# Top-k attention in a hybrid block on Trainium2: one rotation of PSUM pairs, a hold of three slots, six of ten masks on POOL, and checks in groups of three tiles

## The chip, the cores and the metric

One NeuronCore of a Trainium2 chip runs the whole program in one launch. The metric is device time in microseconds (us), lower is better; times given are medians of several executions. Engine names: PE is TensorE (PEld its weight loads), DVE is VectorE, ACT is ScalarE, POOL is GpSimd, SP is SyncE, which issues the DMAs.

## The reference, cut to what matters

The input is 8 images of 64 channels by 56 x 56, so 3136 tokens each. A deformable convolution comes first, then a two-layer top-k self-attention on the 3136 tokens of each image (8 heads of 8 channels, so 64 heads a layer), then a mixture of experts. The change touches the attention alone:

```python
scores = einsum('bhqd,bhkd->bhqk', q, kk) * scale     # 3136 x 3136 per head
vals, idx = top_k(scores, 32)                         # the 32 largest of each row
w = softmax(vals)
out = einsum('bhqk,bhqkd->bhqd', w, take_along_axis(v, idx))
```

## The kernel before, in words

The rows (queries) of a head are cut into 25 tiles of 128 (the last has 64). `heads` runs `attend` in a device loop over blocks of 8 heads: 8 blocks a layer, two layers, so 16 blocks, 128 heads and 3200 tiles. Inside a block each engine has its instructions written out in one fixed order, and semaphores tie the engines together.

A tile goes through these steps:

- **Scores.** PE makes the 3136 scores of the tile in four pieces (`scores`, L271): 2, 2, 2 and 1 matmuls of 448 columns, each piece into the same two PSUM banks 0 and 1. ACT copies each piece to the SBUF ring `S` (`keep`, L400), which holds 8 tiles. PE waits for that copy before the next piece.
- **Selection.** DVE takes the 8 largest of each of 28 chunks of 112 scores (`part_top`, 28 MAX8, L489). Between these, at every second chunk k, it runs one step for the tile before (`candidates`): MAX8 and MATCH_REPLACE8 on 92 candidates (L508 to L521). L521 leaves the 32nd largest score, and its semaphore `found` says so. L525 writes whether a row of the tile may have been selected wrongly.
- **Mask.** A 0/1 mask "score below the threshold" of 128 x 3136 in fp8 is made by the engine that the string `MAKERS` names for tile number mod 10: "D" is one DVE TENSOR_SCALAR right behind L525 (L531), "P" is two POOL instructions after `found`, a comparison into `B` (L214) and a cast into `Z` (L219). `Z` has 10 slots; a mask waits until the mask ten tiles earlier has been read by PE (`mask_freed`).
- **Check.** For a group of tiles (`CHECKS`) PE adds up the doubts into PSUM (`flag`, L279), DVE reads them (L541, L542), loads the maximum into a register and branches. If it isn't zero, DVE searches each flagged tile anew in full rows (`search`, L559 to L566). Until a group is checked its tiles stay in `S`, and the fills that use them wait (`s_free`).
- **Values.** A set is four tiles of queries (512 columns; the seventh set of a head has one tile). For each pair of key tiles, a unit, PE fills two PSUM banks with scores turned round less the row maximum, and adds the masks times a large negative number (`fill`, L309 and L318). ACT takes the exponential (`exps`, L430), PE multiplies with the values (`values`, L354). Units alternate between banks 2 and 3 and banks 4 and 5. The row maxima come by `shift_parts` on POOL (L231 to L236, six small instructions a set, or a tile for the last set), `shifts` on PE and `shift_rows` on ACT.

The order: a block has 800 score pieces (slots) and 640 units, and `units_at(a)` puts 0.8 units behind each slot. Three sets of each block's last head are left over for the next block. PE runs one piece and two units ahead of ACT. The check of a group with last tile L is read by DVE in tile L + 3 at chunk k = 7 (`LATE` is 3), and PE issues its flag before the first piece of tile L + 4. A block ends when every engine has ended.

Of the kernel before, what the change touches and what calls it, by code (L numbers as in the profile page):

```python
# [18 lines left out]
CW = 448  # L19
NC = TOK // CW  # L20
NT = -(-TOK // 128)
# [41 lines left out]
RANKED = TOP_AT + 8 * CHUNKS  # L63
RING = 8
MASKS = 10
MAKERS = "DPDDPDDPDD"
BLOCK = 8
PIECES = (2, 2, 2, 1)
AP = len(PIECES)
# [1 line left out]
SETS = -(-TOK // QW)  # L71
PER_HEAD = 6 * 13 + 2
PENDING = 4
CHECKS = [range(4 * g, 4 * g + 4) for g in range(5)] + [range(20, NT)]
LATE = 3
BEHIND = 4
TERMS, ZERO_TO, MAX_AT = 48, 96, 96


# [26 lines left out]
def attend(nc, m, base, n):  # L106
# [4 lines left out]
    with semaphores(nc, *names) as sems, nc.Block() as block:  # L111
# [10 lines left out]
        units = [(s, p) for s, (i, g) in enumerate(sets) for p in range(len(set_pieces(g)))]  # L122
        NE = len(units)
        SLOTS = NA if n else NE
        first_unit = [next(e for e, (s, _) in enumerate(units) if s == k) for k in range(len(sets))] + [NE]
        batch = [sum(batch_ends(sets[s][1], p) for s, p in units[:e]) for e in range(NE + 1)]

        fold_at = [min(first_unit[s + 1] + 3, first_unit[s + 2]) for s in range(len(sets) - 1)]

        def units_at(a):  # L130

            return range(-(-a * NE // SLOTS), -(-(a + 1) * NE // SLOTS))

        def units_through(i):

# [117 lines left out]

        @block.tensor
        def _(pe):
            def scores(a):
                tile, c = divmod(a, AP)
                i, t = divmod(tile, NT)
                if c == 0:
                    for k in range(len(CHECKS)):  # L260
                        before = tile - LATE - 1 - CHECKS[k][-1]
                        if before >= 0 and before % NT == 0:
                            flag(before // NT, k)
                if t == 0 and c == 0 and i >= 1:
                    pe.wait_ge(q_in, 96 * i)
                if a >= 1:
                    pe.wait_ge(a_ev, a)
                rows = tile_rows(t)
                for j in range(PIECES[c]):
                    at = CW * (sum(PIECES[:c]) + j)  # L270
                    mm = pe.matmul(bank[j][0:rows, 0:CW], m.Q[0:ZERO_TO, side(i), 128 * t:128 * t + rows],  # L271
                                   m.K[0:ZERO_TO, side(i), at:at + CW], start=True, stop=True)
                mm.then_inc(a_mm, 1)

# [18 lines left out]
            def fill(e):  # L293

                s, p = units[e]
                i, g = sets[s]
                w = set_width(g)
                per = QW // w
                if p == 0 and i >= 0:
                    pe.wait_ge(max_in, max_sets(i) + g + 1)  # L300
                    pe.wait_ge(s_free, checks_to(i, set_tiles(g)[-1]))
                    masks_made(pe, NT * i + set_tiles(g)[-1])
                if e >= 2:
                    pe.wait_ge(e_exp, e - 1)

                def shifted(x, k):
                    rows = tile_rows(k)
                    at = w * (x % per)
                    pe.matmul(bank[2 + 2 * (e % 2) + x // per][0:rows, at:at + w],  # L309
                              m.K[0:MAX_AT + 3, side(i), 128 * k:128 * k + rows],  # L310
                              m.Q[0:MAX_AT + 3, side(i), QW * g:QW * g + w], start=True, stop=False)

                def masked(x, k):
                    rows = tile_rows(k)
                    for j, t in enumerate(set_tiles(g)):
                        cols = tile_rows(t)
                        at = w * (x % per) + 128 * j
                        mm = pe.matmul(bank[2 + 2 * (e % 2) + x // per][0:rows, at:at + cols],  # L318
                                       mask_at(NT * i + t)[:, 128 * k:128 * k + rows], m.NEG[:, 0:cols],
                                       start=False, stop=(j == len(set_tiles(g)) - 1))  # L320
                    return mm

                tiles = list(enumerate(set_pieces(g)[p]))
                if per == 1:
                    for x, k in tiles:
                        shifted(x, k)
                    for x, k in tiles:
                        mm = masked(x, k)
                else:
                    for x, k in tiles:  # L330
                        shifted(x, k)
                        mm = masked(x, k)
                mm.then_inc(e_mm, 1)
# [29 lines left out]
                    pe.wait_ge(os_done, s)  # L363
                pe.matmul(psX[0:9, 0:w], m.fold[:, :], m.O4[:, 0:w], start=True, stop=True).then_inc(fold_mm, 1)

            if NA:
                scores(0)
            fill(0)
            fill(1)
            for a in range(SLOTS):  # L370
                if a + 1 < NA:
                    scores(a + 1)
                for e in units_at(a):
                    if e + 2 < NE:
                        fill(e + 2)
                    if e + 4 in first_unit and e + 4 < NE and sets[units[e + 4][0]][0] >= 0:
                        shifts(*sets[units[e + 4][0]])
                    if e in fold_at:
                        fold(fold_at.index(e))
                    if batch_ends(sets[units[e][0]][1], units[e][1]):  # L380
                        values(e)
            for s in range(len(sets)):
                if s == len(sets) - 1 or fold_at[s] >= NE:
                    fold(s)
# [6 lines left out]
        def _(act):  # L391
            def keep(a):
                tile, c = divmod(a, AP)
                i, t = divmod(tile, NT)
                rows, at, w = tile_rows(t), CW * sum(PIECES[:c]), PIECES[c]
                act.wait_ge(a_mm, a + 1)
                if c == 0 and tile >= RING:
                    act.wait_ge(s_free, checks_to(*divmod(tile - RING, NT)))
                    masks_made(act, tile - RING)
                act.copy(m.S[0:rows, slot(tile), at:at + CW * w].rearrange("p (a n) -> p a n", a=w),  # L400
                         m.AB[0:rows, 0:w, 0:CW]).then_inc(a_ev, 1)

            def mask(tile):
                i, t = divmod(tile, NT)
                rows = tile_rows(t)
                act.wait_ge(found, tile + 1)
                if mask_freed(tile):
                    act.wait_ge(e_mm, mask_freed(tile))
                act.activation(mask_at(tile)[0:rows, :], m.S[0:rows, slot(tile), :], ACT.Relu,
                               bias=m.M8[0:rows, side(i), t, 31:32], scale=-1.0).then_inc(z_act, 1)  # L410

            def shift_rows(i, g):
                k = max_sets(i) + g
# [4 lines left out]
            def exps(e):  # L418
                s, p = units[e]
                i, g = sets[s]  # L420
                w = set_width(g)
                tiles, per = set_pieces(g)[p], QW // w
                b = 2 + 2 * (e % 2)
                act.wait_ge(e_mm, e + 1)
                if e >= 4:
                    act.wait_ge(pv, batch[e - 4] + 1)
                whole = [k for k in tiles if tile_rows(k) == 128]
                n_banks = len(whole) // per
                if n_banks:
                    ins = act.activation(m.W[:, e % 4, 0:n_banks, :], m.AB[:, b:b + n_banks, :], ACT.Exp)  # L430
                if len(whole) < len(tiles):
                    rows = tile_rows(tiles[-1])
                    ins = act.activation(m.W[0:rows, e % 4, n_banks, 0:w], m.AB[0:rows, b + n_banks, 0:w], ACT.Exp)  # L433
                ins.then_inc(e_exp, 1)
# [12 lines left out]
                    act.wait_ge(o_out, 16 * (s - 1))  # L447
                act.copy(m.OS[:, s % 2, 0:w], psX[0:9, 0:w]).then_inc(os_done, 1)

            for a in range(SLOTS):  # L450
                if a < NA:
                    keep(a)
                    if a % AP == AP - 1 and a >= AP * BEHIND and maker(a // AP - BEHIND) == "A":
                        mask(a // AP - BEHIND)
                for e in units_at(a):
                    exps(e)
                    if e + 3 in first_unit and e + 3 < NE and sets[units[e + 3][0]][0] >= 0:
                        shift_rows(*sets[units[e + 3][0]])
                    if e - 1 in first_unit[1:]:
                        sums(first_unit.index(e - 1) - 1)  # L460
                    if e - 5 in first_unit[1:]:
                        folded(first_unit.index(e - 5) - 1)
            for tile in range(max(TILES - BEHIND, 0), TILES):
                if maker(tile) == "A":
                    mask(tile)
            sums(len(sets) - 1)
            for s in range(len(sets)):
                if first_unit[s + 1] + 5 >= NE:
# [6 lines left out]
        def _(dve):  # L475
# [93 lines left out]
            for tile in range(TILES):  # L569
                steps = candidates(tile - 1) if tile else []  # L570
                for k in range(CHUNKS):
                    checked = False
                    for g in range(len(CHECKS)):
                        before = tile - LATE - CHECKS[g][-1]
                        if k == 7 and before >= 0 and before % NT == 0:
                            check(before // NT, g)
                            checked = True
                    part_top(tile, k, checked)
# [1310 lines left out]
```

## Time and profile before

| what | value |
|---|---|
| median of 3 runs | 39696.92 us (39691.07 to 39698.17) |
| profiled execution | 39708.52 us, its span 39706.6 us |
| busy | DVE 82%, PE 70%, ACT 54%, POOL 34% |
| mean granted TensorE clock | 0.842 |

The span is the time from the first to the last instruction. Busy time counts an engine's instructions, not its waits on semaphores or its branches. A granted clock of 1.0 is 2.4 GHz, 0.5 is 1.2 GHz. In a timeline, instructions of one line that stand next to each other are merged, with their count; the duration of an instruction overlaps with the start of the next, so distances between starts say more than durations.

### The profile page before, as it was taken

To read this page: it belongs to the slowest core of one execution; us is meant where nothing else is said; L and a number is where in the kernel's file an instruction comes from. 1 tells how busy PE (TensorE), PEld (TensorE's weight loads), DVE (VectorE), ACT (ScalarE), POOL (GpSimd) and SP (SyncE) were. 2 spreads that over 40 slices of the span, in tenths; PEclk is the share of its full clock that TensorE was granted. 3 is DMA by queue.
4 is the path that set the end of the run, shared out by engine and by line. 5 is a ranking of instruction groups with operands and counts; after the bars stand their busy time and mean duration, and the time that the engine had idled before them with its cause. 6 is when DMAs were issued, how large, how long until landed. Compare 5 with 4: busy or idle time off the path is not lost. (4 is left out here: it accounts for less than half of the span.)

```text
span 39706.6 us, 613726 instructions
## 1 busy us (share of the span) xinstructions
PE 27975.2 (70%) x190808; PEld 12251.7 (31%) x190809; DVE 32620.3 (82%) x145784; ACT 21431.0 (54%) x28193; POOL 13534.3 (34%) x7470
## 2 busy tenths in 40 slices
PE   5557776676877767877357677777776777774399
PEld 4533332222333323333123233333332333331122
DVE  5659999999999999999669998989999989996611
ACT  1126665555766656666146566666665666663111
POOL 0004443333444434434024344444443444441000
PEclk7779898888989889989579899999988999896555
DMA  0010000000000000000110000000000000001100
GB/s 37 8 51 5 5 5 4 4 5 4 6 5 5 5 4 6 5 5 5 51 51 5 5 5 5 5 5 5 5 5 4 5 5 5 5 5 42 55 10 7
DMA packets 133124, 454.27 MB, mean 11 GB/s; under 512 B 29244, under 2 KB 85444, under 8 KB 111240
## 3 DMA queue, kind: packets, MB, share of 16 engines
q1 hardware_dynamic: 129256, 410.72, 3.1%
q8 instruction: 1448, 23.72, 0.2%
q14 instruction: 2420, 19.82, 0.2%
HBM read 244.71 MB, written 165.93 MB: 10 GB/s over the span
## 5 line engine op out<-in xcount | busy, mean ns | idle before, releaser
L489 DVE MAX8 C<-S 128x8 f32<-128x112 f32 x89600 | 18969.8, 265 | 1146.0 <-issue 775.5
L400 ACT COPY S<-banks 128x896 f32<-128x896 f32 (+1 forms) x12800 | 10429.5, 815 | 10738.9 <-PE banks L271 7966.3
L214 POOL TENSOR_SCALAR B<-S,M 128x3136 bf16<-128x3136 f32 (+1 forms) x960 | 7894.6, 8224 | 15675.9 <-DVE M L521 15675.9
L271 PE MATMUL banks<-K,Q 96*128 96x448 bf16 x22400 | 6725.9, 371 | 5675.5 <-ACT S L400 5170.6
L430 ACT ACTIVATE W<-banks 128x1024 f32<-128x1024 f32 (+1 forms) x9524 | 9810.9, 1030 | 72.0 <-PE banks L318 71.7
L309 PE MATMUL banks<-Q,K 99*128 99x512 bf16 (+2 forms) x22550 | 6593.2, 378 | 2133.0 <-ACT W L430 2059.6
L354 PE MATMUL banks<-W,V 128*32 128x512 f32 (+1 forms) x45100 | 7188.5, 604 | 145.3 <-ACT W L433 106.2
L318 PE MATMUL banks<-NEG,Z 128*128 128x128 bf16 (+3 forms) x80450 | 6717.5, 227 | 0.0
L318 PEld LDWEIGHTS banks<-NEG,Z 128*128 128x128 fp8e4 (+1 forms) x80450 | 5846.5, 103 | 2570.5 <-issue 463.8
L271 PEld LDWEIGHTS banks<-K,Q 96*128 96x128 bf16 x22400 | 1470.7, 99 | 12174.3 <-ACT S L400 7731.6
L531 DVE TENSOR_SCALAR Z<-S,M 128x3136 fp8e4<-128x3136 f32 (+1 forms) x2240 | 4694.9, 2096 | 31.1 <-PE banks L318 31.1
L219 POOL CAST Z<-B 128x3136 fp8e4<-128x3136 bf16 (+1 forms) x960 | 3693.0, 3847 | 138.9 <-POOL B L214 8.5
L309 PEld LDWEIGHTS banks<-Q,K 99*128 99x128 bf16 (+1 forms) x22550 | 1787.9, 103 | 5384.2 <-ACT W L430 3745.9
L517 DVE MATCH_REPLACE8 C<-M,C 128x92 f32<-128x92 f32 x9600 | 2266.6, 236 | 2.3 <-issue 0.5
L516 DVE MAX8 M<-C 128x8 f32<-128x92 f32 x9600 | 2262.2, 236 | 1.7
L354 PEld LDWEIGHTS banks<-W,V 128*32 128x32 f32 x45100 | 1284.3, 114 | 1080.6 <-issue 508.1
L1734 DVE TENSOR_TENSOR moe_hw<-moe_hg,banks 128x448 f32<-128x448 f32 x448 | 278.4, 621 | 1514.1 <-ACT moe_hg L1667 1514.1
L865 PE MATMUL banks<-dc_tap,c_group 128*128 128x224 f32 x2800 | 777.0, 362 | 789.5 <-DVE dc_tap L920 789.5
L541 DVE CAST FI<-banks 1x4 int32<-1x4 f32 (+1 forms) x768 | 118.9, 155 | 1376.4 <-PE banks L279 1373.9
L1667 ACT ACTIVATE moe_hg<-banks,moe_b 128x448 f32<-128x448 f32 x448 | 284.0, 634 | 1563.9 <-PE banks L1629 1563.9
L885 ACT ACTIVATE dc_d<-banks,c_omb 128x224 f32<-128x224 f32 x378 | 149.6, 448 | 1801.5 <-PE banks L854 1801.3
L561 DVE MAX8 M<-S 128x8 f32<-128x3136 f32 (+1 forms) x297 | 1018.0, 3427 | 23.8 <-issue 2.3
(200 smaller groups left out, 21734.9 us busy)
## 6 DMA issues: line engine op xcount, KB each, us to landing
q<-ln_o SPq DMA_DIRECT2D x20, 1568.0 KB, 5.1
ln_x<-y SPq DMA_DIRECT2D x16, 1568.0 KB, 6.0
K<-k_parts SPq DMA_DIRECT2D x130, 147.0 KB
Q<-q_parts SPq DMA_DIRECT2D x130, 147.0 KB
q_parts<-pj_parts SPq DMA_DIRECT2D x24, 784.0 KB, 4.7
k_parts<-pj_parts SPq DMA_DIRECT2D x24, 784.0 KB, 7.8
V<-v_rows SPq DMA_DIRECT2D x130, 112.5 KB, 7.4
v_rows<-pj_vt SPq DMA_DIRECT2D x8, 1800.0 KB, 11.8
```

The lines of the kernel that those rows point to most:

```text
L214: chained(lambda: pool.tensor_scalar(m.B[0:rows, :], m.S[0:rows, slot(tile), :], m.M8[0:rows, side(i), t, 31:32], None, ALU.is_lt))
L219: pool.tensor_copy(mask_at(tile)[0:rows, :], m.B[0:rows, :], saturate=False).then_inc(z_pool, 1)
L271: mm = pe.matmul(bank[j][0:rows, 0:CW], m.Q[0:ZERO_TO, side(i), 128 * t:128 * t + rows], m.K[0:ZERO_TO, side(i), at:at + CW], start=True, ...
L309: pe.matmul(bank[2 + 2 * (e % 2) + x // per][0:rows, at:at + w], m.K[0:MAX_AT + 3, side(i), 128 * k:128 * k + rows], m.Q[0:MAX_AT + 3, sid ...
L318: mm = pe.matmul(bank[2 + 2 * (e % 2) + x // per][0:rows, at:at + cols], mask_at(NT * i + t)[:, 128 * k:128 * k + rows], m.NEG[:, 0:cols], ...
L354: mm = pe.matmul(psO[32 * (k % 4):32 * (k % 4) + 32, 0:w], m.V1[0:rows, side(i), k, :], m.W[0:rows, at, x // per, w * (x % per):w * (x % p ...
L400: act.copy(m.S[0:rows, slot(tile), at:at + CW * w].rearrange("p (a n) -> p a n", a=w), m.AB[0:rows, 0:w, 0:CW]).then_inc(a_ev, 1)
L430: ins = act.activation(m.W[:, e % 4, 0:n_banks, :], m.AB[:, b:b + n_banks, :], ACT.Exp)
L489: ins = dve.max(m.C[0:rows, tile % 2, TOP_AT + k:RANKED:CHUNKS], m.S[0:rows, slot(tile), CHUNK * k:CHUNK * k + CHUNK])
L516: steps.append(lambda r=r: chained(lambda: dve.max(top(r), few)))
L517: steps.append(lambda r=r: chained(lambda: dve.match_replace(few, top(r), few, LOW)))
L531: dve.tensor_scalar(mask_at(tile)[0:rows, :], m.S[0:rows, slot(tile), :], m.M8[0:rows, side(i), t, 31:32], None, ALU.is_lt, saturate=False ...
```

## The change

The scores and the units no longer have banks of their own. `works` lists pieces and units in the order in which ACT takes them, and work w uses banks 2(w mod 3) and the next one; PE produces work w + 3 when work w has been read. The units of a block stand three slots later (`HOLD`). `MAKERS` goes from 3 POOL masks in ten to 6. Checks go from six groups of four tiles a head (the last of five) to eight of three (the last of four), are read at chunk k = 14, and their flag is issued before the third piece of tile L + 3. ACT's own mask path, which no letter of `MAKERS` used, is gone.

```diff
-MAKERS = "DPDDPDDPDD"
+MAKERS = "DPPDPDPPDP"
-CHECKS = [range(4 * g, 4 * g + 4) for g in range(5)] + [range(20, NT)]
+CHECKS = [range(3 * g, 3 * g + 3) for g in range(7)] + [range(21, NT)]
 LATE = 3
-BEHIND = 4
+HOLD = 3
+PAIRS_ = 3
...
+        DELAY = HOLD if n else 0
...
         def units_at(a):
-
-            return range(-(-a * NE // SLOTS), -(-(a + 1) * NE // SLOTS))
+            a -= DELAY
+            return range(-(-max(a, 0) * NE // SLOTS), -(-max(a + 1, 0) * NE // SLOTS))
+
+        works = []
+        for a in range(SLOTS + DELAY):
+            works += [("score", a)] * (a < NA) + [("value", e) for e in units_at(a)]
...
+        def pair(w):
+            return 2 * (w % PAIRS_)
...
+            def freed(w):
+                if w >= PAIRS_:
+                    kind, x = works[w - PAIRS_]
+                    pe.wait_ge(a_ev if kind == "score" else e_exp, x + 1)
...
-                if c == 0:
+                if c == 2:
                     for k in range(len(CHECKS)):
-                        before = tile - LATE - 1 - CHECKS[k][-1]
+                        before = tile - LATE - CHECKS[k][-1]
...
-                if a >= 1:
-                    pe.wait_ge(a_ev, a)
+                freed(score_at[a])
...
-                if e >= 2:
-                    pe.wait_ge(e_exp, e - 1)
+                freed(value_at[e])
...
+            for w in range(PAIRS_):
+                produce(w)
+            for w, (kind, e) in enumerate(works):
+                produce(w + PAIRS_)
+                if kind == "value":
                     if e in fold_at:
                         fold(fold_at.index(e))
                     if batch_ends(sets[units[e][0]][1], units[e][1]):
                         values(e)
+                    if e + 5 in first_unit and e + 5 < NE and sets[units[e + 5][0]][0] >= 0:
+                        shifts(*sets[units[e + 5][0]])
...
-                        if k == 7 and before >= 0 and before % NT == 0:
+                        if k == 14 and before >= 0 and before % NT == 0:
```

## Rows read from the trace of the kernel before

**Rows 1.** The page, part 5: groups by line; busy us, mean ns, idle before.

```profile
L489 DVE MAX8 C<-S 128x8 f32<-128x112 f32 x89600 | 18969.8, 265 | 1146.0 <-issue 775.5
L531 DVE TENSOR_SCALAR Z<-S,M 128x3136 fp8e4<-128x3136 f32 (+1 forms) x2240 | 4694.9, 2096 | 31.1 <-PE banks L318 31.1
L561 DVE MAX8 M<-S 128x8 f32<-128x3136 f32 (+1 forms) x297 | 1018.0, 3427 | 23.8 <-issue 2.3
```

**Rows 2.** Waits of the whole span: total us, times, longest.

```profile
ACT S L400 <- PE banks L271: 7966.3, 7064, 3.8
PE banks L271 <- ACT S L400: 5170.6, 3452, 81.0
DVE FI L541 <- PE banks L279: 1373.9, 612, 5.7
DVE C L489 <- ACT S L400: 250.8, 184, 10.8
```

**Rows 3.** Line L489 in each layer: count, min/median/max ns, first and last start.

```profile
L489 DVE MAX8 C<-S x44800: 252/265/288, 2884.4 to 18845.5; 128x8 f32<-128x112 f32 x192, 64x8 f32<-64x112 f32 x8
...
L489 DVE MAX8 C<-S x44800: 252/265/288, 20383.3 to 36103.4; 128x8 f32<-128x112 f32 x192, 64x8 f32<-64x112 f32 x8
```

**Rows 4.** Busy time by engine in one stretch of attention.

```profile
25000.00:30000.00 5000.00, 3862.75 (x28852) 1639.27 (x28852) 4567.38 (x22242) 3309.55 (x4238) 2191.15 (x1218) 0.92 0.02 5
```

**Rows 5.** DVE timeline, two thresholds, a POOL-masked and a DVE-masked tile, a check.

```profile
26362.38 0.24 DVE L521 MAX8 M<-C 128x8 f32<-128x92 f32 x1
...
26369.08 0.24 DVE L521 MAX8 M<-C 128x8 f32<-128x92 f32 x1
...
26370.12 2.46 DVE L531 TENSOR_SCALAR Z<-S,M 128x3136 fp8e4<-128x3136 f32 x1
...
26377.20 0.14 DVE L542 TENSOR_REDUCE FI<-banks 1x1 int32<-1x4 f32 x1
26378.53 0.28 DVE L489 MAX8 C<-S 128x8 f32<-128x112 f32 x1 [1.19 <-issue]
...
26382.51 1.83 DVE L531 TENSOR_SCALAR Z<-S,M 128x3136 fp8e4<-128x3136 f32 x1
26384.26 1.51 DVE L489 MAX8 C<-S 128x8 f32<-128x112 f32 x8
```

**Rows 6.** POOL timeline beside it, and the cast of an earlier mask.

```profile
26315.28 2.80 POOL L219 CAST Z<-B 128x3136 fp8e4<-128x3136 bf16 x1
...
26362.72 8.21 POOL L214 TENSOR_SCALAR B<-S,M 128x3136 bf16<-128x3136 f32 x1 [17.45 <-DVE M L521]
26371.06 4.16 POOL L219 CAST Z<-B 128x3136 fp8e4<-128x3136 bf16 x1
26375.20 0.23 POOL L231 TENSOR_SCALAR R<-M 128x4 f32<-128x4 f32 x1
...
26376.56 0.19 POOL L236 CAST P<-R 128x4 bf16<-128x4 f32 x1
```

**Rows 7.** POOL timeline where a mask came late.

```profile
8581.59 8.23 POOL L214 TENSOR_SCALAR B<-S,M 128x3136 bf16<-128x3136 f32 x1 [11.40 <-DVE M L521]
8589.95 2.80 POOL L219 CAST Z<-B 128x3136 fp8e4<-128x3136 bf16 x1
```

**Rows 8.** DVE timeline in the same place.

```profile
8590.09 4.30 DVE L531 TENSOR_SCALAR Z<-S,M 128x3136 fp8e4<-128x3136 f32 x1 [1.01 <-PE banks L318]
```

**Rows 9.** DVE timeline of a search.

```profile
25174.63 0.14 DVE L542 TENSOR_REDUCE FI<-banks 1x1 int32<-1x4 f32 x1
...
25205.75 0.28 DVE L489 MAX8 C<-S 128x8 f32<-128x112 f32 x1 [2.81 <-issue]
```

**Rows 10.** DVE timeline at the end of a block.

```profile
26268.88 0.25 DVE L521 MAX8 M<-C 64x8 f32<-64x92 f32 x1
...
26281.61 1.52 DVE L489 MAX8 C<-S 128x8 f32<-128x112 f32 x8 [8.37 <-ACT S L400]
```

**Rows 11.** POOL timeline there, its last instruction of the block.

```profile
26272.40 0.19 POOL L236 CAST P<-R 128x1 bf16<-128x1 f32 x1
```

More of the change, by code:

```diff
@@ L130, in units_at @@
         def units_at(a):
-            return range(-(-a * NE // SLOTS), -(-(a + 1) * NE // SLOTS))
+            a -= DELAY
[3 more added lines that the diff above has]
+            works += [("score", a)] * (a < NA) + [("value", e) for e in units_at(a)]
+        score_at = {x: w for w, (kind, x) in enumerate(works) if kind == "score"}
+        value_at = {x: w for w, (kind, x) in enumerate(works) if kind == "value"}
+        def pair(w):
+            return 2 * (w % PAIRS_)
         def units_through(i):
@@ L270, in scores @@
                     at = CW * (sum(PIECES[:c]) + j)
-                    mm = pe.matmul(bank[j][0:rows, 0:CW], m.Q[0:ZERO_TO, side(i), 128 * t:128 * t + rows],
+                    mm = pe.matmul(bank[pair(score_at[a]) + j][0:rows, 0:CW], m.Q[0:ZERO_TO, side(i), 128 * t:128 * t + rows],
                                    m.K[0:ZERO_TO, side(i), at:at + CW], start=True, stop=True)
@@ L302, in fill @@
                     masks_made(pe, NT * i + set_tiles(g)[-1])
-                if e >= 2:
-                    pe.wait_ge(e_exp, e - 1)
+                freed(value_at[e])
+                b = pair(value_at[e])
                 def shifted(x, k):
@@ L308, in shifted @@
                     at = w * (x % per)
-                    pe.matmul(bank[2 + 2 * (e % 2) + x // per][0:rows, at:at + w],
+                    pe.matmul(bank[b + x // per][0:rows, at:at + w],
                               m.K[0:MAX_AT + 3, side(i), 128 * k:128 * k + rows],
@@ L317, in masked @@
                         at = w * (x % per) + 128 * j
-                        mm = pe.matmul(bank[2 + 2 * (e % 2) + x // per][0:rows, at:at + cols],
+                        mm = pe.matmul(bank[b + x // per][0:rows, at:at + cols],
                                        mask_at(NT * i + t)[:, 128 * k:128 * k + rows], m.NEG[:, 0:cols],
@@ L364, in fold, with produce @@
                 pe.matmul(psX[0:9, 0:w], m.fold[:, :], m.O4[:, 0:w], start=True, stop=True).then_inc(fold_mm, 1)
[L366 to L377, printed above, removed]
+            def produce(w):
+                if w < len(works):
+                    kind, x = works[w]
+                    if kind == "score":
+                        scores(x)
+                    else:
+                        fill(x)
+            for w in range(PAIRS_):
[3 more added lines that the diff above has]
+                if kind == "value":
                     if e in fold_at:
@@ L400, in keep @@
                 act.copy(m.S[0:rows, slot(tile), at:at + CW * w].rearrange("p (a n) -> p a n", a=w),
[L401 to L410, printed above, removed]
+                         m.AB[0:rows, pair(score_at[a]):pair(score_at[a]) + w, 0:CW]).then_inc(a_ev, 1)
             def shift_rows(i, g):
@@ L422, in exps @@
                 tiles, per = set_pieces(g)[p], QW // w
-                b = 2 + 2 * (e % 2)
+                b = pair(value_at[e])
                 act.wait_ge(e_mm, e + 1)
@@ L448, in folded @@
                 act.copy(m.OS[:, s % 2, 0:w], psX[0:9, 0:w]).then_inc(os_done, 1)
[L450 to L465, printed above, removed]
+            for kind, x in works:
+                if kind == "score":
+                    keep(x)
+                    continue
+                exps(x)
+                if x + 4 in first_unit and x + 4 < NE and sets[units[x + 4][0]][0] >= 0:
+                    shift_rows(*sets[units[x + 4][0]])
+                if x - 1 in first_unit[1:]:
+                    sums(first_unit.index(x - 1) - 1)
+                if x - 5 in first_unit[1:]:
+                    folded(first_unit.index(x - 5) - 1)
             sums(len(sets) - 1)
```

## The prediction, made before the changed kernel ran

> **What bounds the kernel now.** I read the page first, then the waits, then the timelines of DVE and POOL. The two attention layers run from 2884.4 to 18845.5 and from 20383.3 to 36103.4, together 31,682 us of the span, 9.90 us for each of 3200 tiles [rows 3]. Nothing outside them changes. DVE is the fullest engine there, 4567 of 5000 us in a stretch where PE has 3863 and ACT 3310 [rows 4].
>
> DVE's time adds up from rows. Let F(t) be the start of the threshold MAX8 (L521) of tile t. With no mask by DVE between, F to F is 26369.08 - 26362.38 = 6.70 us [rows 5], so 3200 tiles take 21,440. The 2240 DVE masks (Z from here on) have 4694.9 us busy, and the next instruction starts 0.08 before such a mask's end (26382.51 + 1.83 against 26384.26): 4516 [rows 1, 5]. A check costs 0.08 between its two reads and 1.33 until the next MAX8, 1.41; 768 of them are 1083 [rows 5]. DVE waits 1374 us for flags from PE [rows 2]. The sum is 28,413. A search adds 31.12 - 1.33 = 29.8 us, and there were 297 / 3 = 99, so 2950 [rows 1, 9]. The remaining 319 us are 16 blocks starting and ending.
>
> The flag wait says who else is near the bound: PE makes a piece only after ACT has copied the piece before, and the waits between the two, 7966 and 5171 us, show this handing to and fro [rows 2]. So before there are two limits close together: DVE's own 27,039 and the pace of PE and ACT, which adds 1374.
>
> **What goes.** Three pairs of banks in rotation let PE be three works ahead. PE and ACT then need at most their busy time: that is 77% and 66% of 9.90, at most 7.65 and 6.55 us a tile [rows 4], below DVE's. The flag comes two pieces earlier and is read seven chunks later. I cost the flag wait at 0 (bounds: 0, and 1.79 us for each of 1024 checks if nothing improves). The cover is PE's lead of about 1.3 us a tile; without it the wait is back. DVE masks fall from 7 to 4 in ten: 960 fewer, which at 1.75 alone are 1680 us less.
>
> **What comes: POOL and DVE shut each other out.** This term decides. POOL's comparison B starts at 26362.72 and ends at 26370.93. Z is issued at 26370.12, inside it, and ends at 26372.58: 1.65 us after B's end, where a Z alone takes 1.83 [rows 5, 6]. So Z did nothing until B was over. The cast behind takes 4.16 instead of 2.80 [rows 6], for it waits for Z in turn. Z in another place is issued 0.14 us after a cast began and takes 4.30; it ends 1.64 after the cast's end, so it waited for all of it [rows 7, 8]. MAX8 shows nothing of the kind: between F and F with B running it keeps the 6.70. Today the loss is small by luck of timing: Z comes 7.40 us after B's start, when B has 0.8 left.
>
> No row shows a Z issued early in a B. Bounds: at least 0.63 us (2.46 - 1.83) [rows 5], at most the rest of B. I take the whole rest, since the cast showed a whole wait.
> The Trainium skill, SBUF — State Buffer, section Who interferes with whom, says that VectorE in a two-port mode and GpSimd take one port pair exclusively, and that the one that is later blocks for the other's whole instruction. The trace agrees for the end of B and for the whole cast; for an early Z this rule gives the upper bound, and the sum below is what it makes of the change.
>
> The new MAKERS repeats every five tiles, as does the head of 25: D P P D P. Two P in a row are what hurts. Five tiles, without checks:
> - F1: B1 starts 0.34 later, its cast 8.34 after that and takes 2.80. B2 is ready but queued; it starts 0.14 after the cast, at F1 + 11.62, and ends at 19.84. F3 is at 13.40 and Z3 is issued 1.04 later, at 14.44. It waits for B2 and ends at 21.49. The next instruction starts 0.08 before, and from the end of a Z to the next F it is 6.70 - 1.04 = 5.66. F4 = F1 + 27.07.
> - F4 to F6: B4 ends at F4 + 8.56, Z5 (issued at 7.74) at 10.21, and F6 = F4 + 15.79.
> Sum 42.86 for five tiles, 8.57 a tile; with each Z alone it would be 5 x 6.70 + 2 x 1.75 = 37.0. POOL is then 3 x 11.3 us busy of 43, so it isn't the bound itself; its queue only puts B2 where Z3 falls.
>
> Checks stand between F(L+1) and F(L+2) for L = 2, 5, 8, 11, 14, 17, 20, 24. By place in the five: three lie between F1 and F3, where Z3 would have waited anyway, and cost 0; four lie before an F1 or between F3 and F4 and cost 1.41; the one between F9 and F10 (L = 8) makes Z10 miss B's end and hit the cast, so F9 to F11 becomes 0.34 + 8.34 + 2.80 + 1.65 - 0.08 + 5.66 = 18.71, costing 2.92. Together 8.56 a head.
> The shift work on POOL is 1.4 + 0.2 = 1.6 us a set (26375.20 to the end of the one at 26376.56) [rows 6]. For the set that ends with tile 11, a first P of a pair, it stands between cast and B12 and delays Z13 by 1.6. The other sets' shifts fall where POOL has room.
> A head: 5 x 42.86 + 8.56 + 1.6 = 224.5, times 128 is 28,730, against 28,413 before: +317.
>
> **Smaller terms.**
> - Searches stay 99, since the data set them. During one POOL empties its queue, so the next Z doesn't wait: with B2 only started after it (L = 5 and 20) F1 to F4 is 3 x 6.70 + 1.41 + 2.38 = 23.9 instead of 27.07, 3.2 less; with B2 done in it (L = 11) 23.3, 3.8 less; for L = 8 the Z is alone, 2.2 less. At 3/25 of the tiles for each group that is about 1.5 a search: -150.
> - A block's last tile (199) was D and is P now. Behind its threshold at 26268.88 POOL ended at 26272.40 + 0.19, and the next block's MAX8 came at 26281.61 [rows 10, 11]. Now B and cast (0.34 + 8.34 + 2.80) come first, then a shift of 1.6: POOL ends at some 26282.0, 9.5 later, with nothing beside it. 16 blocks: +152. Bounds 0 and 11.5 each.
> - The hold adds three slots' worth of units after a block's last piece, about 2.4 units on PE and ACT, while POOL makes the last masks: 0.
> - The hold, the shifts (one unit earlier) and the longer way of the POOL masks tighten the mask slots. Z10 of a head waits until PE has filled set 0 (13 units, 4.06 tiles of slots). That fill needs the check of tiles 3 to 5, now read in tile 8, about 1 us before F7. From there to Z10 it is 1.0 + (27.07 - 8.11) + 9.15 = 29.1 us, and Z10 loses nothing until 31.4, the end of the cast it waits for. 4.06 x 7.65 = 31.1 us fits, barely: 0, with a bound of 5 us a head. Z18 and Z30 have more room.
>
> **Sum.** +317 - 150 + 152 = +319. On the profiled execution's 39708.5 (2 us over its span) that is 40,028; on the median of 39696.9, which is 12 us lower, 40,016. I forecast 40,020. Own range 39,600 to 40,500: 0.1 us a tile either way is 320 us.
>
> **Rivals.**
> 1. Much faster: Z slips into B early. If POOL gives way inside a long B, every Z costs at most 1.75 + 0.63. A head is 25 x 6.70 + 10 x 2.38 + 8 x 1.41 = 202.6, times 128 is 25,930, so -2480 + 152: 37,370. For it: no row shows a wait inside B longer than its last 0.8 us. Against: the 4.30 us Z [rows 8], which waited for a whole cast.
> 2. Slower than the forecast: PE and ACT keep their old pace of some 8.9 us a tile (28,413 / 3200). Then set 0's fill takes 36.1 us where 31.4 are covered, and Z10 holds DVE 4.7 us in each head: +600, 40,620. It decides from a pace over 7.7. For it: PE is 77% busy now and stops at every fill whose check is late. Against: three pairs, and ACT at 6.55.
> 3. The checks still wait for their flag. 1024 x 1.79, of which the 5/8 that stand in no lock wait count: +1150, 41,170. Against: flag earlier, read later, both by some 2 us or more.
> That the change is slower at all is the forecast's own case; rival 1 is the one on the other side.
>
> **How the numbers follow.** Chances: forecast 0.70, rival 1 0.15, rival 2 0.12, rival 3 0.03. A difference under 0.2% (80 us) can't be told from none here. Of the forecast's 0.70, 0.51 lies over 0.2% slower, 0.11 within, 0.08 below, since the sum is a small rest of two large terms. Faster 0.15 + 0.08 = 0.23, same 0.11, slower 0.51 + 0.12 + 0.03 = 0.66. The range reaches from 39,450 to 40,900; outside lie rival 1, rival 3 and a little of the forecast's ends, 0.2 together.
>
> **What the profile after would show.** Z (L531) 1280 times with a mean near 4.5 us: half of them at 5.6 to 8.7 us (issued in the second B of a pair), most others at 2.46, some at 3.9. B stays at 8.22. The flag wait at L541 falls from 1374 us to under 200. The MAX8 spacing stays 6.70 a tile. The time between blocks grows by 9 to 10 us. I'm wrong on the deciding step if Z's mean is under 2.6 (rival 1), and on the cover if L531 waits for PE or L489 for ACT by hundreds of us (rival 2), or if L541 still waits over 1000 us (rival 3).

## The result, and the profile after

The changed kernel takes 40118.69 us (median of 4 runs, 40118.19 to 40119.29) against 39697.54: ratio 1.0106, 95% interval [1.0088, 1.0123], 421 us slower. The forecast was 40,020. The profiled span is 40116.6 us, at a mean granted TensorE clock of 0.792 (0.842 before). The clock doesn't order these kernels: two experiments below are at 0.843 and 0.816, the first slower than the kernel before and the second the fastest of all.

The groups of the page after; columns as in [rows 1]. L535 is the DVE mask that was L531, L225 and L230 are POOL's comparison and cast.

```profile
L225 POOL TENSOR_SCALAR B<-S,M 128x3136 bf16<-128x3136 f32 (+1 forms) x1920 | 15768.7, 8213 | 8010.2 <-DVE M L525 7923.9
L493 DVE MAX8 C<-S 128x8 f32<-128x112 f32 x89600 | 18766.9, 264 | 1172.3 <-issue 746.0
L535 DVE TENSOR_SCALAR Z<-S,M 128x3136 fp8e4<-128x3136 f32 x1280 | 5851.4, 4571 | 288.5 <-PE banks L333 287.1
```

DVE makes 960 masks fewer and spends more time on them: 5851 us for 1280, where it was 4695 for 2240 [rows 1]. The mean went from 2096 to 4571 ns, while a comparison on POOL is as long as before.

DVE's waits after, as in [rows 2]:

```profile
DVE Z L535 <- PE banks L333: 287.1, 193, 3.2
...
DVE FI L545 <- PE banks L294: 209.1, 16, 13.1
...
DVE C L493 <- ACT S L418: 121.7, 16, 9.5
```

The flag wait fell from 1374 us in 612 waits to 209 in 16, one at each block's end. That half of the change works. The wait for mask slots has grown (287, before 31 [rows 1]).

Here is one pair of POOL masks, in DVE's timeline after. The L525 are the thresholds of tiles 6, 7, 8, 9 and 11; that of tile 10 (26191.77) is left out.

```profile
26156.48 0.23 DVE L525 MAX8 M<-C 128x8 f32<-128x92 f32 x1
...
26164.40 0.24 DVE L525 MAX8 M<-C 128x8 f32<-128x92 f32 x1
26171.11 0.23 DVE L525 MAX8 M<-C 128x8 f32<-128x92 f32 x1
26172.15 5.79 DVE L535 TENSOR_SCALAR Z<-S,M 128x3136 fp8e4<-128x3136 f32 x1
26183.53 0.23 DVE L525 MAX8 M<-C 128x8 f32<-128x92 f32 x1
...
26192.81 3.86 DVE L535 TENSOR_SCALAR Z<-S,M 128x3136 fp8e4<-128x3136 f32 x1
26202.26 0.23 DVE L525 MAX8 M<-C 128x8 f32<-128x92 f32 x1
```

And POOL beside it:

```profile
26156.81 8.20 POOL L225 TENSOR_SCALAR B<-S,M 128x3136 bf16<-128x3136 f32 x1 [7.57 <-DVE M L525]
26165.14 2.80 POOL L230 CAST Z<-B 128x3136 fp8e4<-128x3136 bf16 x1
26168.10 8.21 POOL L225 TENSOR_SCALAR B<-S,M 128x3136 bf16<-128x3136 f32 x1 [0.16 <-POOL Z L230]
26176.43 4.16 POOL L230 CAST Z<-B 128x3136 fp8e4<-128x3136 bf16 x1
26183.87 8.22 POOL L225 TENSOR_SCALAR B<-S,M 128x3136 bf16<-128x3136 f32 x1 [1.76 <-DVE M L525]
26192.22 2.80 POOL L230 CAST Z<-B 128x3136 fp8e4<-128x3136 bf16 x1
```

The second comparison starts behind the first cast, at 26168.10, and ends at 26176.31. The DVE mask issued at 26172.15, in its middle, ends at 26177.94, 1.63 us after it. From threshold 6 to threshold 9 it is 27.05 us; the prediction's cycle said 27.07. The mask of 26192.81 was pushed behind its comparison's end by a check and waited for the cast: 18.73 us for that stretch, forecast 18.71.

### The profile page after: what moved, and what is told of

Same layout as the page of the kernel before. It is cut to its first block and busy times, and to the rows that moved or that the text cites. A ratio compares the mean times of both kernels' runs of the same rounds, so it can differ in the third digit from the quotient of the medians.

```text
span 40116.6 us, 618786 instructions
## 1 busy us (share of the span) xinstructions
PE 27369.4 (68%) x191320; PEld 12412.4 (31%) x191321; DVE 33909.2 (85%) x145336; ACT 21346.2 (53%) x28193; POOL 23729.4 (59%) x9390
## 5 line engine op out<-in xcount | busy, mean ns | idle before, releaser
L225 POOL TENSOR_SCALAR B<-S,M 128x3136 bf16<-128x3136 f32 (+1 forms) x1920 | 15768.7, 8213 | 8010.2 <-DVE M L525 7923.9
L493 DVE MAX8 C<-S 128x8 f32<-128x112 f32 x89600 | 18766.9, 264 | 1172.3 <-issue 746.0
L418 ACT COPY S<-banks 128x896 f32<-128x896 f32 (+1 forms) x12800 | 10233.8, 818 | 4910.6 <-PE banks L286 2842.2
L324 PE MATMUL banks<-Q,K 99*128 99x512 bf16 (+2 forms) x22550 | 6748.5, 385 | 4737.9 <-issue 3563.6
L369 PE MATMUL banks<-W,V 128*32 128x512 f32 (+1 forms) x45100 | 6970.7, 589 | 108.7 <-ACT W L442 79.0
L230 POOL CAST Z<-B 128x3136 fp8e4<-128x3136 bf16 (+1 forms) x1920 | 6726.4, 3503 | 267.1 <-POOL B L225 6.9
L535 DVE TENSOR_SCALAR Z<-S,M 128x3136 fp8e4<-128x3136 f32 x1280 | 5851.4, 4571 | 288.5 <-PE banks L333 287.1
L324 PEld LDWEIGHTS banks<-Q,K 99*128 99x128 bf16 (+1 forms) x22550 | 1783.6, 103 | 9504.0 <-issue 5471.7
L286 PEld LDWEIGHTS banks<-K,Q 96*128 96x128 bf16 x22400 | 1699.0, 102 | 3944.4 <-ACT S L418 2732.3
L294 PE MATMUL banks<-VI,c_ones 128*1 128x3 f32 (+1 forms) x2048 | 195.7, 166 | 2691.6 <-DVE VI L529 2689.5
L369 PEld LDWEIGHTS banks<-W,V 128*32 128x32 f32 x45100 | 1160.2, 114 | 2029.9 <-issue 1729.0
```

Of the source, the lines that this page charges most:

```text
L225: chained(lambda: pool.tensor_scalar(m.B[0:rows, :], m.S[0:rows, slot(tile), :], m.M8[0:rows, side(i), t, 31:32], None, ALU.is_lt))
L230: pool.tensor_copy(mask_at(tile)[0:rows, :], m.B[0:rows, :], saturate=False).then_inc(z_pool, 1)
L286: mm = pe.matmul(bank[pair(score_at[a]) + j][0:rows, 0:CW], m.Q[0:ZERO_TO, side(i), 128 * t:128 * t + rows], m.K[0:ZERO_TO, side(i), at:at ...
L324: pe.matmul(bank[b + x // per][0:rows, at:at + w], m.K[0:MAX_AT + 3, side(i), 128 * k:128 * k + rows], m.Q[0:MAX_AT + 3, side(i), QW * g:Q ...
L369: mm = pe.matmul(psO[32 * (k % 4):32 * (k % 4) + 32, 0:w], m.V1[0:rows, side(i), k, :], m.W[0:rows, at, x // per, w * (x % per):w * (x % p ...
L493: ins = dve.max(m.C[0:rows, tile % 2, TOP_AT + k:RANKED:CHUNKS], m.S[0:rows, slot(tile), CHUNK * k:CHUNK * k + CHUNK])
```

## The experiments

Each ran in three rounds against the kernel before; times are medians. The kernel before took 39,697 to 39,700 us every time, so times are compared across experiments too.

**Rotation, hold and new checks, with the old MAKERS.**

```diff
-MAKERS = "DPPDPDPPDP"
+MAKERS = "DPDDPDDPDD"
```

> The changed kernel with the old MAKERS (3 POOL masks in ten, never two in a row); rotation, hold and checks of three stay. Lock theory (the changed kernel lost its gain because a POOL mask queued behind another one is still being compared when DVE issues its own): no DVE mask is then issued early in a POOL comparison. DVE adds up to 21440 + 4516 + 1024 x 1.41 = 27,400 us in the attention against 28,413 before, plus 100 to 300 for masks that a check pushes into a cast: 38,800 to 39,100. DVE masks at 2.46 or 3.9 us or less, none at 5 and over. Rival (the rotation gives nothing, PE and ACT keep 8.9 us a tile): 39,700 or more, DVE waiting for PE.

39276.28 us, ratio 0.9894 [0.9877, 0.991]. So the change without its new mask split is 421 us faster than before, and the split on top costs 842. It is some 180 us more than the top of what I expected: DVE waits 530 us for mask slots, which I hadn't put in.

**The new MAKERS alone, in the kernel before.**

> The kernel before with only the new MAKERS (6 POOL masks in ten, in pairs); banks, order and checks stay as before. Lock theory: a head takes 214.3 us plus checks 7.2 plus shift 1.6, times 128 is 28,550, plus the flag waits that stand outside a lock wait (0 to 900 us), plus 152 at the block ends: 39,990 to 40,900, though DVE runs 960 masks fewer. Masks of DVE at 5.6 to 7.1 us in half of the cases. Rival (the lock costs little, the rotation or the hold is what costs): DVE has 1680 us less work and PE and ACT set the pace as before: 38,000 to 39,700.

39987.21 us, ratio 1.0072 [1.0056, 1.0089], 3 us below my range. The split makes the kernel slower without rotation, hold or new checks, by 290 us, at a granted clock of 0.843. Its DVE masks take nearly as long as in the changed kernel, 4261 ns in the mean (there 4571):

```profile
L531 DVE TENSOR_SCALAR Z<-S,M 128x3136 fp8e4<-128x3136 f32 x1280 | 5453.5, 4261 | 24.8 <-PE banks L318 23.8
```

Here it costs less than on top of the rotation, for the flag wait also shrinks, from 1374 to 809 us; I read this as PE catching up while DVE is held at its mask. The rotation as the culprit is out.

**The changed kernel with six checks of four tiles.**

```diff
-CHECKS = [range(3 * g, 3 * g + 3) for g in range(7)] + [range(21, NT)]
+CHECKS = [range(4 * g, 4 * g + 4) for g in range(5)] + [range(20, NT)]
```

> The changed kernel with CHECKS in six groups of four, as before; all else as changed. Two checks a head fewer. By the places of the checks in the pattern of five (a check inside a lock wait is free) they cost 7.2 us a head instead of 8.6, 180 us in all: 39,940. If the late check of tiles 3 to 5 is what makes the DVE masks wait for PE (287 us of waits, and up to 1.1 us more each for hitting the cast), that goes too: down to 39,600. If the wait for mask slots comes from the hold and not from the checks, it stays and the time is 39,900 to 40,000. Rival (the number of checks is nothing): 40,120.

40176.17 us, ratio 1.012 [1.0103, 1.0137]: 57 us slower than the changed kernel, not 180 faster. A miss. 256 checks of some 1.4 us are gone, and the masks took the time back:

```profile
L535 DVE TENSOR_SCALAR Z<-S,M 128x3136 fp8e4<-128x3136 f32 x1280 | 6040.4, 4719 | 371.7 <-PE banks L333 371.5
```

They are busy 189 us longer and wait 84 us longer for slots. In the trace the checks lie where I had counted them; waits for mask slots ate the gain. One of them is POOL's:

```profile
POOL Z L230 <- PE banks L333: 137.0, 123, 2.0
```

It is the cast of tile 1's mask: it waits for its slot in 123 of the 128 heads, which starts the second comparison 0.87 us later, and so the mask of tile 3 takes 7.9 us (7.1 in the changed kernel). DVE's mask of tile 10 waits 1.4 us a head for its slot and then meets a cast, 2.94 us lost; in the changed kernel that loss is at tile 5 (below). In heads without a search the 25 tiles take 226.8 us, against 227.0 in the changed kernel, where I had expected 1.4 less. That is 25 us in all; the 80 us that are lost outside those heads I haven't placed. The size of the check groups, the part that the change's name speaks of, moves little.

**POOL's comparison cut short.** The first 392 of 3136 columns are compared, the rest is left out; B is set to zero once at the start. Most masks of POOL are then empty and the results wrong.

```diff
-                chained(lambda: pool.tensor_scalar(m.B[0:rows, :], m.S[0:rows, slot(tile), :],
+                chained(lambda: pool.tensor_scalar(m.B[0:rows, 0:392], m.S[0:rows, slot(tile), 0:392],
```

> The changed kernel with POOL's comparison cut to 392 of 3136 columns (the rest of B stays zero, so six masks in ten are mostly empty); everything else runs as changed. Lock theory: no DVE mask meets a comparison any more, each takes 1.83 us; a head is 25 x 6.70 + 10 x 1.75 + 8 x 1.41 = 196.3 us, times 128 is 25,130, 3600 less than the forecast of the changed kernel: 36,400 to 36,800. Rival (PE and ACT are the limit near 8.9 us a tile in the changed kernel too): 39,000 to 39,700. In between, some 37,500, if PE and ACT need about 8.2 us a tile.

37244.0 us, ratio 0.9381 [0.9365, 0.9396]: 2875 us less than the changed kernel, though DVE has the same instructions and even eight searches more (107 for 99, all eight in the second layer, whose input the wrong masks change).

```profile
L225 POOL TENSOR_SCALAR B<-S,M 128x392 bf16<-128x392 f32 (+1 forms) x1920 | 2429.4, 1265 | 18040.3 <-DVE M L525 18037.7 <-issue 2.5
...
L535 DVE TENSOR_SCALAR Z<-S,M 128x3136 fp8e4<-128x3136 f32 x1280 | 2422.6, 1893 | 718.8 <-PE banks L333 718.6
```

The same 1280 masks fell from 5851 to 2423 us. The gain is smaller than those 3429 us, since 432 us more of waiting for mask slots came in their place. With the eight searches that is also why the time is above 36,800.

**The changed kernel without the hold.**

```diff
-HOLD = 3
+HOLD = 0
```

> The changed kernel with HOLD = 0: the units stand three slots earlier, as before the change. In the changed kernel the mask of each head's tile 5 waits 1.7 us for PE to free its mask slot and then falls into a cast (3.54 us instead of 2.45), 2.8 us a head. Theory (the hold makes PE late with the slots): three slots are some 6.7 us, the wait is gone, 39,760. Rival (the wait comes from the rotation's order and the late check, and PE now stops at fills whose masks or check are not ready): 40,100 to 40,300.

40180.36 us, ratio 1.0121 [1.0104, 1.0138]. The time lies in the rival's range, though the theory's mechanism is there: the slot wait is gone (6 us) and masks are 406 us shorter. But DVE now waits for pieces:

```profile
DVE C L493 <- ACT S L418: 826.8, 704, 9.4
```

In the changed kernel that is 122. PE's idle time before fills (L324) that the profile lays to no engine grew beside it, from 3564 to 5421 us, so I read the hold as a trade: a wait for slots against a stop of PE at fills. For this kernel the two are worth about the same.

**Alternating makers: five in ten by POOL, never two in a row.**

```diff
-MAKERS = "DPPDPDPPDP"
+MAKERS = "PDPDPDPDPD"
```

> The changed kernel with MAKERS PDPDPDPDPD: five POOL masks in ten, never two in a row. Lock theory: each DVE mask comes 7.4 us after a comparison began and takes 2.46, or 3.9 when a check stands between; 21440 + 1600 x 2.38 + 1024 x 1.41 + 240 for the casts hit is 26,930, and 300 to 600 of waits for mask slots as in the run with the old MAKERS (530): 38,500 to 38,900, though only one POOL mask in ten is less than in the changed kernel (40,119). Rival (any POOL share over three in ten costs): 39,300 to 40,100.

38989.76 us, ratio 0.982 [0.9804, 0.9837]. One POOL mask in ten fewer than in the changed kernel, and 1129 us less. The mean DVE mask is 2763 ns. Slot waits are 704 us, which is why it is 90 above my range.

**Alternating, and the DVE mask 3.65 us later.** The mask leaves `candidates` and becomes the sixth step of the next tile's list. `late_mask`, whose definition is left out here, holds the same wait and the same instruction as `mask` did:

```diff
-MAKERS = "DPPDPDPPDP"
+MAKERS = "PDPDPDPDPD"
...
-                return steps + [final, doubt] + ([mask] if maker(tile) == "D" else [])
+                return steps + [final, doubt]
...
                 steps = candidates(tile - 1) if tile else []
+                steps[5:5] = [lambda: late_mask(tile - 2)]
...
+                late_mask(TILES - 2)
                 for remaining in candidates(TILES - 1):
                     remaining()
+                late_mask(TILES - 1)
```

> The alternating kernel, and each DVE mask moved from behind its own tile's L529 to the fifth candidate step of the next tile (chunk 11), 4.1 us later, when POOL's cast has just ended and the next comparison has not begun. Lock theory: every DVE mask takes 1.83, no cast is stretched; 21440 + 1600 x 1.75 + 1444 = 25,680 plus 0 to 400 of slot waits: 37,000 to 37,400. Rival (what is left is PE's and ACT's pace, seen as 8.1 us a tile in the run with the short comparison): 37,400 to 37,900 with DVE waiting for PE or ACT. If the lock is no matter of timing: as the alternating kernel.

36937.08 us, ratio 0.9305 [0.9289, 0.932], the fastest of all, 7% under the kernel before and 63 us below my range, at a granted clock of 0.816. (The move is 3.65 us by the trace, 4.69 behind the threshold; I had written 4.1.) POOL, and DVE beside it:

```profile
26049.18 8.21 POOL L225 TENSOR_SCALAR B<-S,M 128x3136 bf16<-128x3136 f32 x1 [5.23 <-DVE M L525]
26057.52 2.80 POOL L230 CAST Z<-B 128x3136 fp8e4<-128x3136 bf16 x1
```

```profile
26055.55 0.23 DVE L525 MAX8 M<-C 128x8 f32<-128x92 f32 x1
26060.24 1.83 DVE L541 TENSOR_SCALAR Z<-S,M 128x3136 fp8e4<-128x3136 f32 x1
```

The cast ends at 26060.32, the mask is issued 0.08 before and takes 1.83. Over the span:

```profile
L230 POOL CAST Z<-B 128x3136 fp8e4<-128x3136 bf16 (+1 forms) x1600 | 4496.2, 2810 | 213.2
L541 DVE TENSOR_SCALAR Z<-S,M 128x3136 fp8e4<-128x3136 f32 (+1 forms) x1600 | 2995.2, 1872 | 99.8 <-PE banks L333 99.2
```

Against the run before it, 1425 us of mask time and 604 us of slot waits are gone; a later mask also finds its slot free more often.

**The same without the hold.**

> The kernel before it in this call (alternating, late DVE mask) with HOLD = 0. If slot waits are left there and come from the hold, it is faster by them, 100 to 400 us. If they are gone by the later mask, or if the fills now wait for masks, the same or slower by up to 200 us.

37617.61 us, ratio 0.9476 [0.946, 0.9492], 680 slower than with the hold; I had expected at most 200. DVE waits 819 us for pieces from ACT. Where the lock no longer slows DVE, the hold is worth 1.8%.

**The late mask in the changed kernel, with its own MAKERS.**

> The changed kernel with its own MAKERS (two POOL masks in a row), and only the DVE mask moved 3.65 us later (issued 4.69 us behind the threshold instead of 1.04). Lock theory: the mask of tile 3 of five is issued at F1 + 18.1, when the second comparison has 1.7 us left, ends at 21.49 as now, but 2.0 us and not 5.7 then remain to the next threshold; the other one falls just behind a cast. Five tiles take 38.6 us instead of 42.9, a head 201.6, times 128 is 25,800 against 28,730: 37,200, up to 37,600 with waits for slots. Rival (the loss is the POOL queue itself, whatever the moment of the DVE mask): 39,500 to 40,100.

37337.18 us, ratio 0.9406 [0.939, 0.9421]: 2782 us off the changed kernel, by moving one instruction in its engine's order. Number, kind and size of all instructions, and the POOL queue with its pairs, stay.

```profile
L541 DVE TENSOR_SCALAR Z<-S,M 128x3136 fp8e4<-128x3136 f32 x1280 | 3328.5, 2600 | 7.4 <-PE banks L333 7.1
```

**Alternating and late in the kernel before, without rotation, hold and new checks.**

> The kernel before with MAKERS PDPDPDPDPD and the late DVE mask; banks, order, hold and checks as before. If PE's and ACT's old handing to and fro is a limit of its own at some 8.9 us a tile, DVE's 2700 us less work turn into waits for flags and pieces: 39,300 to 39,900. If it was only the flag's place, or the rotation is worth nothing: near 36,940, as with the rotation.

39690.16 us, ratio 0.9997 [0.9987, 1.0007]. No difference. DVE's masks take 1869 ns in the mean there, 1704 us less in all than before, and the flag wait takes it back:

```profile
DVE FI L546 <- PE banks L279: 2795.9, 693, 7.3
```

It is 1422 us longer than before, and the wait for pieces from ACT 211 us longer (462 for 251). So the pace of PE and ACT with scores in one pair of banks is a limit of its own, at the time of the kernel before. The rotation with its hold, its earlier flags and its later, smaller checks lifts it: 36,937 against 39,690 with the same masks. Which of these parts does how much wasn't separated, but for the hold (above); an earlier flag without the rotation wasn't tried.

## Why the prediction was right

- **The lock.** The deciding step held in mechanism and in size. Of the 1280 DVE masks in the trace after, 998 were issued in a comparison, with 0.73 to 6.35 us of it left, and every one ended 1.64 to 1.65 us behind its end; the longest took 8.00 us. The forecast mean was near 4.5 us; it is 4.57. The short comparison takes 3429 us of mask time away, the late mask 2523. Rival 1 is refuted.
- **The cycle.** 27.05 and 18.73 us measured for 27.07 and 18.71 worked out.
- **The flag wait.** Costed at 0, and 0 inside the blocks. Rival 3 is refuted. The 209 us at the block ends lie beside POOL's last mask, which was in the sum.
- **Block ends.** Threshold to next block was 12.73 us [rows 10]. In the changed kernel these lines follow each other on DVE:

```profile
28463.38 0.25 DVE L525 MAX8 M<-C 64x8 f32<-64x92 f32 x1
28476.99 0.16 DVE L545 CAST FI<-banks 1x4 int32<-1x4 f32 x1 [13.07 <-PE banks L294]
28485.56 2.57 DVE L493 MAX8 C<-S 128x8 f32<-128x112 f32 x14 [8.34 <-ACT S L418]
```

  That is 22.18, 9.45 more, forecast 9.5. But a block's first tile is quicker, which the sum has at nothing. Its first MAX8 and its threshold, before (26281.61 [rows 10]) and after (28485.56):

```profile
26296.67 0.23 DVE L521 MAX8 M<-C 128x8 f32<-128x92 f32 x1
```

```profile
28495.16 0.24 DVE L525 MAX8 M<-C 128x8 f32<-128x92 f32 x1
```

  15.06 us became 9.60, as DVE no longer waits for the pieces of that tile (behind the first, 2.64, 0.49, 0.37 and 0.91 us before). Over the 16 blocks the medians are 14.4 and 9.6: some 77 us back of the 152.
- **Slots, the step that failed.** "Z18 and Z30 have more room" was wrong for Z30, which is tile 5 of the next head and takes the slot of tile 20. Where this head meets it:

```profile
26137.75 0.24 DVE L525 MAX8 M<-C 128x8 f32<-128x92 f32 x1
26144.45 0.24 DVE L525 MAX8 M<-C 128x8 f32<-128x92 f32 x1
26147.34 3.54 DVE L535 TENSOR_SCALAR Z<-S,M 128x3136 fp8e4<-128x3136 f32 x1 [1.77 <-PE banks L333]
```

  Thresholds 4 and 5, then a wait of 1.77 us for the slot, then the cast. From threshold 4 to threshold 6 (26156.48) it is 18.73 us where I had 15.79: 2.94 a head, 376 us in all. Every head is like it: the mask of tile 5 waits in all 128, 218 us of the 287, and from its threshold to the next it is 12.03 us in the mean, where 9.09 were costed. The run without the hold shows the cause: there the wait is gone. Z10, which I feared, waits little (24 us in 24 heads), Z18 45 us in 37.
- **The sum.** +319 forecast, +421 measured. The missed 376 are more than the difference of 102, so other terms were some 270 us too dear, and that the total lies so close is in part luck. Three of them can be placed in the trace after. The blocks' first tiles give the 77 us above. A head without a search takes 227.0 us, where 224.5 and 2.9 for the slot make 227.4: some 50 us. A search costs some 27.5 us over the same tiles without one, where the sum has 29.8 less 1.5: some 80 us. The last 70 or so stay open.
- **Rival 2** is not what happened, though its sign came up: L535 waits for PE by hundreds of us, 287. Without the hold that wait is 6 us, and with the late masks the same rotation runs at 36,937 us, so it is the hold and not the pace of PE and ACT. Its place, a mask slot, was the right kind of place.

## What to carry to other kernels

Work moved from DVE to POOL is not off DVE's path if DVE's remaining masks and POOL's instructions can't run together: count how long each would hold the other at the moment it is issued, not their busy shares. Then look for the gap: 3.65 us later for one instruction was worth 2782 us, where the size of the check groups moved 57. And two limits that lie close together hide each other's cures: alternating late masks without the rotation gave nothing, the rotation with hold and checks 1.1%, both 7.0%.

## What the runs showed of the hardware

- A DVE TENSOR_SCALAR from f32 to fp8 of 128 x 3136 (1.83 us alone) waits for the end of a comparison or cast of POOL that is under way: in the trace after, all 998 issued in a comparison and 246 in a cast ended 1.64 to 1.65 us behind it (1.74 at most, where under 0.2 us of it was left). The other way round, the cast at 26176.43, begun while the mask ran, took 4.16 us for 2.80. POOL's small shift instructions never met a mask, so for them nothing is shown.
- MAX8 runs beside them unhindered: threshold 7 to threshold 8 took 6.71 us while POOL's second comparison began. In the trace after, MAX8 of 112 columns that stand next to each other start 0.176 us apart in the median, the same beside a comparison, beside a cast and beside neither.
- POOL's comparison from f32 takes 8.21 us for 3136 columns and 1.27 for 392; its cast of 3136 columns from bf16 to fp8 only 2.80, a third.
